# Softmax in a fused image-text block: the row maximum subtracted on VectorE, head by head, in place of one GpSimd operation

## The chip, the cores and the metric

The kernel runs on one core of a Trainium2 chip. The core has five engines that run their own instruction streams and meet only at semaphores: PE (TensorE, matrix products), DVE (VectorE), ACT (ScalarE), POOL (GpSimd) and SP (SyncE, which here only issues transfers). The time is device time in microseconds (us) of one execution; the median of three runs is 970.14 us, the lowest 968.85 and the highest 973.57.

## What is computed

64 samples. Each has 36 image tokens (a patch embedding with shifted copies, then a layer norm) and 77 text tokens, so T = 113 tokens of width 128. One attention layer of 8 heads and one mixture of 16 experts (3 for each token) with a shared expert follow, both with a residual. What matters here is the softmax inside the attention:

```
h = layernorm_patches(x);  h = concat([h, txt], axis=1)            # (64, 113, 128)
q, k, v = projections of layernorm(h), 8 heads of 64
scores = (q * scale) @ k.T        -> bfloat16                       # (64, 8, 113, 113)
probs  = softmax(scores)          -> bfloat16                       # subtract the row maximum, exp, divide
h = h + (probs @ v) @ Wo + bo
h = h + shared_expert(layernorm(h)) + sum over the 3 chosen experts of gate * expert(layernorm(h))
```

## The kernel before, in words

It has three stages. Up to some 120 us the image tokens are made. From some 120 to 620 us a software pipeline runs over the samples, which is the stage of the change. After it, 100 tiles of 256 expert rows are computed and the results are gathered and added.

**The pipeline.** `steps` writes the same step out for each engine: octets of 8 samples, k = 0 to 7 in each, six of the octets in a loop. Sample n = 8 o + k is the one whose softmax stands in the step. In the same step other parts work on other samples: the layer norm of n + 8 (L1137), the projections of n + 4, the scores and v of n + 1, the product of probabilities and v of n - 1 (L715 to L717), the output projection (L687), the residual (L1148) and the second layer norm (L1150, L1161, L498, L500, L1188) of n - 2, the gate of n - 3. Each engine takes its instructions in the order in which they are written, and a wait holds all behind it.

**The softmax of a sample.** ScalarE copies the scores from two PSUM banks into `s16` as bfloat16 (L890, `s_copied`). VectorE takes the maximum of each row and head (L1142, `max_done`). GpSimd subtracts it, all 8 heads in one operation, with the maximum broadcast along a row (L488, `sub_done`). ScalarE takes the exponential into `p16` (L884). TensorE transposes the 8 heads (L650), ScalarE copies them out (L855), and TensorE multiplies by v.

**VectorE's step** in order: xn of n + 8 (L1137); the maximum (L1142); the residual add of n - 2, which waits for TensorE's output projection L687 (L1148); statistics (L1150); a correction of the transposed input (L1155); the statistics' end (L1161); the reciprocal of the softmax sum, which waits for the last product L717 (L1169); the division (L1171); v's remainders (L1177, L1182); the rows to be sent (L1188), which wait for GpSimd's L500. TensorE's L715 waits for L1148, since both use one PSUM bank. Between these stand pieces of the routing: the choice of experts for four samples in the steps with k % 4 == 3 and 0 (L1026 to L1065), their places in the steps with k % 4 == 1 (L1077 to L1088).

**GpSimd's step** in order: the subtraction (L488), a bias add to `h` (L494), the reciprocal root of the second norm (L498, L500, after L1161), and 0, 3, 3, 3, 3, 4, 4, 4 indirect transfers (L533, table `SENDS`), which send the previous octet's rows to their experts. Octet 0 has none of these.

Of the kernel before, what the change touches and what calls it, by code (L numbers as in the profile page):

```python
# [15 lines left out]
BF16 = mybir.dt.bfloat16  # L16
U32 = mybir.dt.uint32
I32 = mybir.dt.int32
ALU = mybir.AluOpType
# [41 lines left out]
def build(nc, x, txt, w_main, w_sx, w_sy, tok_bias, tok_gb, wq, wkv, wo, bo, gate_w, e_bias, w_ffn, out):  # L61
    ctx = ExitStack()
    with ctx:
        def sb(name, shape, dt=FP32):
            return ctx.enter_context(nc.sbuf_tensor(name, shape, dt))
# [76 lines left out]
        v1 = [top_half(vf[i][0:T, :, :]) for i in range(4)]  # L142
        v2 = [top_half(vr[i][0:T, :, :]) for i in range(4)]

        s16 = [sb(f"s16_{i}", [128, H, T], BF16) for i in range(2)]
        p16 = [sb(f"p16_{i}", [128, H, T], BF16) for i in range(2)]
        mx = [sb(f"mx{i}", [128, H], BF16) for i in range(2)]
        pt = [sb(f"pt{i}", [128, H, 128], BF16) for i in range(2)]
        rec = sb("rec", [128, 2, H])

# [90 lines left out]
        def after(eng, name, n, plus=1):  # L241

            if isinstance(n, int) and n + plus <= 0:
                return
            eng.wait_ge(S[name], n + plus)
# [42 lines left out]
        def ok(n, end=B):  # L288

            return not isinstance(n, int) or 0 <= n < end  # L290
# [104 lines left out]
        def _(pool):  # L395
# [84 lines left out]
            def step(o, k):  # L480
                n = o * OCT + k
                if isinstance(o, int) and o == -1 and k in (4, 5):
                    first_rs(NOCT - 2 if k == 4 else NOCT - 1)
                if ok(n):


                    after(pool, "max_done", n)
                    nc.gpsimd.tensor_tensor(s16[k % 2][0:T, :, :], s16[k % 2][0:T, :, :],  # L488
                                            mx[k % 2][0:T, :].unsqueeze(2).to_broadcast([T, H, T]), ALU.subtract).then_inc(S["sub_done"], 1)
                if ok(n + 6):  # L490

                    after(pool, "xn_ready", n + 6)
                    hn = h[0:T, bass.ds(n + 6, 1), :].rearrange("p a d -> p (a d)")
                    nc.gpsimd.tensor_tensor(hn, hn, bo_sb[0:T, :], ALU.add).then_inc(S["hb_done"], 1)  # L494
                if ok(n - 2):

                    after_all(pool, ("ones_set", 5), ("st2_done", n - 2, 1))
                    nc.gpsimd.tensor_scalar(ve2[0:T, k % 2:k % 2 + 1], mv2[0:T, k % 2, 1:2], EPS, None, ALU.add).then_inc(S["ve2_done"], 1)  # L498
                    after(pool, "ve2_done", n - 2)
                    nc.gpsimd.tensor_tensor(rs2[0:T, k % 2:k % 2 + 1], ve2[0:T, k % 2:k % 2 + 1], half[0:T, 0:1], ALU.pow).then_inc(S["rs2_done"], 1)  # L500
                send(o, k, 0)
                send(o, k, 1)

                if ok(n - 7) and k % GRP == GRP - 1:

                    q, half_ring = o * 2 + (k - 7) // GRP, (k - 7) % OCT // GRP
                    at = slice(half_ring * GRP, (half_ring + 1) * GRP)
                    if not isinstance(q, int) or q >= 1:
                        after(pool, "dest_set", 2 * q, 0)
                    for j in range(GRP):  # L510
                        b = half_ring * GRP + j
                        reuse(pool, b, o - 1 if k < 7 else o)
                    nc.gpsimd.tensor_tensor(pay[0:T, at, :, ROW - 1].bitcast(I32), dest_i[0:T, :, :], dzero[0:T, :, :], ALU.add).then_inc(S["dest_set"], 1)
                    after(pool, "dest_set", 2 * q)
                    nc.gpsimd.tensor_tensor(dest_i[0:T, :, :], dest_i[0:T, :, :], dstep[0:T, :, :], ALU.add).then_inc(S["dest_set"], 1)
                send(o, k, 2)
# [44 lines left out]
        def _(pe):  # L561
# [43 lines left out]


            pe.wait_ge(S["z_copied"], NOCT)
            pe.wait_ge(S["pt_zero"], 3)
            pe.wait_ge(S["ones_set"], 5)

            def shared_hidden(g, gate_bank, up_bank):
# [193 lines left out]
        def _(act):  # L805
# [22 lines left out]
                    copies(j * 2 + i, i)  # L828
                    image_rows(act, j * 2 + i - 2, i)

            act.wait_ge(S["pt_zero"], 3)

            def early(g, i):
                if ok(g, NEARLY):
# [4 lines left out]
            def step(o, k):  # L839
# [40 lines left out]
                if ok(n):  # L880

                    after(act, "sub_done", n)
                    after(act, "pt_done", n, -1)
                    nc.scalar.activation(p16[k % 2][0:T, :, :], s16[k % 2][0:T, :, :], ACT.Exp).then_inc(S["exp_done"], 1)  # L884
                if ok(n + 1):

                    after(act, "s_done", n + 1)
                    after(act, "exp_done", n + 1, -1)
                    for i in range(2):
                        m = nc.scalar.activation(s16[(k + 1) % 2][0:T, i:H:2, :], bank[3 + i][0:T, 0:4 * T].rearrange("p (c t) -> p c t", t=T),  # L890
                                                 ACT.Copy)
                    m.then_inc(S["s_copied"], 1)
                if isinstance(o, int) and o == NOCT and k == IDLE:
# [55 lines left out]
        def _(dve):  # L949
# [56 lines left out]
            for i in range(2):  # L1006
                nc.vector.memset(pt[i][:, :, :], 0.0).then_inc(S["pt_zero"], 1)
            nc.vector.memset(bank[5][:, :], 0.0).then_inc(S["pt_zero"], 1)
            dve.wait_ge(S["pt_zero"], 3)
            dve.wait_ge(S["iota_f"], 5)  # L1010

            def per_choice(a):
# [111 lines left out]
            def step(o, k):  # L1124
# [14 lines left out]
                if ok(n):  # L1139

                    after(dve, "s_copied", n)
                    nc.vector.reduce_max(mx[i][0:T, :], s16[i][0:T, :, :], AX.X).then_inc(S["max_done"], 1)  # L1142
                routing(o, k, 0)
                if ok(n - 2):

# [156 lines left out]
```

## Time and profile before

| | |
|---|---|
| median of three runs | 970.14 us |
| the profiled execution | 973.1 us |
| its span | 971.3 us |
| PE busy | 703.8 us (72%) |
| DVE busy | 599.2 us (62%) |
| ACT busy | 440.4 us (45%) |
| POOL busy | 676.2 us (70%) |
| granted TensorE clock, mean | 0.865 |

The profiled execution is one run with the hardware profiler on; its span is the time from its first to its last instruction, and 1.8 us lie around it. Busy is the time in which an engine has at least one instruction in work. The shares are means over stages with different limits, so the stage of the pipeline is read by itself below.

### The profile page before, as it was taken

The numbers are of one execution on the slowest core, as the hardware profiler recorded it, in microseconds if no ns is written. First come the engines' busy times: TensorE is split into PE (matmuls) and PEld (weight loads), VectorE is DVE, ScalarE is ACT, GpSimd is POOL, SyncE is SP. The second block draws the span as 40 slices with busy tenths as digits, with TensorE's granted clock in tenths as the row PEclk, the third lists the DMA queues.
The fourth block names the chain that finished last, engine by engine and source line by source line (L and its number), as shares of the span: only waits on it lengthen the run. The fifth ranks groups of instructions, "written<-read, shape, count | busy, mean of one in ns | idle before, by whom it ended". The sixth has DMA issues, their size and how long they took to land.

```text
span 971.3 us, 21625 instructions
## 1 busy us (share of the span) xinstructions
PE 703.8 (72%) x6192; PEld 578.9 (60%) x6192; DVE 599.2 (62%) x1659; ACT 440.4 (45%) x1027; POOL 676.2 (70%) x782
## 2 busy tenths in 40 slices
PE   3472599987988879888797788589887777877000
PEld 2362377876777768767676677458665655655000
DVE  1197578777887987888778786534333333333095
ACT  2121388666766757666666665214333223332000
POOL 2169354687887887878778777755777777777553
PEclk9686699888998998999899886589999999999555
DMA  7540000000000000000000000157666565663196
GB/s 197 163 136 19 12 1 2 18 26 19 22 27 17 24 27 19 25 19 24 24 19 24 20 24 28 34 169 216 197 185 175 176 184 166 176 182 118 49 349 214
DMA packets 71473, 85.60 MB, mean 88 GB/s; under 512 B 13943, under 2 KB 65152, under 8 KB 71355
## 3 DMA queue, kind: packets, MB, share of 16 engines
q1 hardware_dynamic: 33912, 37.34, 13.5%
q10 hardware_dynamic: 24976, 25.32, 9.4%
q0 software_dynamic: 12544, 22.44, 6.9%
q8 instruction: 19, 0.31, 0.1%
q14 instruction: 22, 0.18, 0.1%
HBM read 55.50 MB, written 31.85 MB: 90 GB/s over the span
## 4 chain that ended last, share of the span: by engine, by line
issue 26%; POOL 24%; PE 18%; DMA 8%; DVE 8%; ACT 1%; POOLq 1%; DVEq 0%; SPq 0%
POOL dispatched L533 8%; POOL expert_rows L546 7%; POOL s L488 6%; DMA expert_rows<-yb,xs_all 5%; PE bank L603 4%; PE bank L687 3%; DMA x2t<-expert_rows 3%; PE bank L735 2%; PE bank L650 2%; PE bank L703 2%; POOL h L494 2%; POOL rs L500 1%; DVE h L1255 1%; PE bank L783 1%; ACT p L884 1%
## 5 line engine op out<-in xcount | busy, mean ns | idle before, releaser
L546 POOL DMA_INDIRECT expert_rows<-yb,xs_all x200 | 194.4, 972 | 73.2 <-issue 51.8
L533 POOL DMA_INDIRECT dispatched<-pay,sloti x192 | 198.3, 1033 | 62.0 <-issue 58.4
L488 POOL TENSOR_TENSOR s<-s,mx 113x904 bf16<-113x904 bf16 x64 | 109.3, 1708 | 45.0 <-DVE mx L1142 44.4
L1243 DVE TENSOR_TENSOR yb<-bank,xs_all 128x256 f32<-128x256 f32 x100 | 42.3, 423 | 142.8 <-DMA expert_rows<-yb,xs_all 140.8
L603 PE MATMUL bank<-xt,wqkv 128*128 128x452 f32 x384 | 114.4, 434 | 1.2 <-DVE xt L1155 0.7
L783 PE MATMUL bank<-xe,kt 128*128 128x256 f32 x400 | 105.3, 386 | 0.1
L921 ACT ACTIVATE xe<-bank 128x256 f32<-128x256 f32 x100 | 38.3, 383 | 140.2 <-PE bank L771 132.9
L792 PE MATMUL bank<-kt,hide 128*128 128x128 f32 x400 | 67.2, 291 | 47.6 <-DVE hide L1233 47.0
L792 PEld LDWEIGHTS bank<-kt,hide 128*128 128x128 f32 x400 | 55.3, 191 | 73.8 <-DVE hide L1233 60.9
L884 ACT ACTIVATE p<-s 113x904 bf16<-113x904 bf16 x64 | 61.3, 957 | 53.8 <-POOL s L488 53.5
L603 PEld LDWEIGHTS bank<-xt,wqkv 128*128 128x128 f32 x384 | 77.5, 220 | 7.3 <-DVE xt L1155 0.9
L650 PE MATMUL bank<-ident,p 113*113 113x113 bf16 x512 | 42.8, 232 | 46.7 <-ACT p L884 46.6
L687 PEld LDWEIGHTS bank<-wo_r,ot 128*113 128x113 f32 x512 | 72.8, 211 | 5.7 <-ACT ot L850 2.0
L783 PEld LDWEIGHTS bank<-xe,kt 128*128 128x128 f32 x400 | 68.8, 192 | 7.1 <-issue 0.7
L687 PE MATMUL bank<-wo_r,ot 128*113 128x128 f32 x512 | 70.4, 288 | 1.5 <-ACT ot L850 1.5
L1142 DVE TENSOR_REDUCE mx<-s 113x8 bf16<-113x904 bf16 x64 | 69.5, 1087 | 2.2 <-ACT s L890 1.9
L735 PE MATMUL bank<-kt,qt 64*113 64x113 f32 x1024 | 70.5, 279 | 0.0
L703 PE MATMUL bank<-wqkv,xt 128*113 128x512 f32 x192 | 66.1, 456 | 0.1
L650 PEld LDWEIGHTS bank<-ident,p 113*113 113x113 bf16 x512 | 35.1, 143 | 51.6 <-ACT p L884 51.2
L715 PEld LDWEIGHTS bank<-vf,pt 113*128 113x128 bf16 x512 | 49.1, 101 | 26.5 <-issue 26.5
L735 PEld LDWEIGHTS bank<-kt,qt 64*113 64x113 f32 x1024 | 58.8, 183 | 8.0 <-issue 2.1
L890 ACT ACTIVATE s<-bank 113x452 bf16<-113x452 f32 x128 | 62.4, 543 | 2.6 <-PE bank L735 2.4
(161 smaller groups left out, 1799.4 us busy)
## 6 DMA issues: line engine op xcount, KB each, us to landing
kt<-in_w_ffn ACTq DMA_DIRECT2D x100, 192.0 KB
xs_all<-dispatched SPq DMA_DIRECT2D x100, 130.0 KB, 2.5
x2t<-expert_rows SPq DMA_DIRECT2D x16, 672.0 KB
x2t<-in_x SPq DMA_DIRECT2D x8, 864.0 KB, 5.6
out_h<-h ACTq DMA_DIRECT2D x16, 224.0 KB
expert_rows<-yb,xs_all POOLq DMA_INDIRECT x200, 2.3
dispatched<-pay,sloti POOLq DMA_INDIRECT x192, 2.3
h<-in_txt SPq DMA_DIRECT2D x1, 2464.0 KB
```

The costliest lines, as they stand in the source:

```text
L488: nc.gpsimd.tensor_tensor(s16[k % 2][0:T, :, :], s16[k % 2][0:T, :, :], mx[k % 2][0:T, :].unsqueeze(2).to_broadcast([T, H, T]), ALU.subtra ...
L533: pool.indirect_dma_start(out=xs_dram[:, :], out_offset=bass.IndirectOffsetOnAxis(ap=sloti[:, b // GRP, b % GRP, c:c + 1], axis=0), in_=pa ...
L546: pool.indirect_dma_start(out=y_dram[:, :], out_offset=bass.IndirectOffsetOnAxis(ap=xs[slot][:, j, ROW - 1:ROW].bitcast(I32), axis=0), in_ ...
L603: m = nc.tensor.matmul(dst, wqkv[:, a, at:at + 128], xg[:, b, :], start=(j == 0), stop=(j == 2))
L650: m = nc.tensor.transpose(ptp[0:T, hh * 128:hh * 128 + T], p16[(k - 1) % 2][0:T, hh, :], ident16[0:T, 0:T])
L687: m = nc.tensor.matmul(bank[7][0:T, 0:D], ot[k % 2][:, c, :], wo_r[:, a, c * D:(c + 1) * D], start=(c == a == 0), stop=(c == NC - 1 and a ...
L703: m = nc.tensor.matmul(bank[1][0:T, :], xt[gv][:, b, kv * T:(kv + 1) * T], wqkv[:, a, 2 * H * DH:], start=(j == 0), stop=(j == 2))
L735: m = nc.tensor.matmul(bank[3 + e][0:T, c * T:(c + 1) * T], qt[gs][half_p, c, ks * T:(ks + 1) * T], kt[gs][half_p, c, ks * T:(ks + 1) * T] ...
L783: m = nc.tensor.matmul(bank[3 - i][:, j * TR:(j + 1) * TR], w_ex[slot][:, j * F:(j + 1) * F], xe[1 - i][:, :], start=True, stop=True)
L792: m = nc.tensor.matmul(bank[4 + i][:, j * D:(j + 1) * D], hide[i][:, j * 128:(j + 1) * 128], w_ex[(k - 2) % RW][:, 2 * F:], start=True, st ...
L884: nc.scalar.activation(p16[k % 2][0:T, :, :], s16[k % 2][0:T, :, :], ACT.Exp).then_inc(S["exp_done"], 1)
L1142: nc.vector.reduce_max(mx[i][0:T, :], s16[i][0:T, :, :], AX.X).then_inc(S["max_done"], 1)
```

## The change

The scores' tile gets 114 columns for each head instead of 113, and column 113 is set to zero once ahead of the pipeline. The row maximum is kept as 32-bit numbers. GpSimd's subtraction goes. In its place VectorE, after the maximum and a wait for it, issues eight operations, one for each head, on 113 partitions and 114 bfloat16 elements, with the head's maximum as a scalar of each partition. The last of them signals `sub_done`. ScalarE's copies and exponential leave the added column out.

```
-        s16 = [sb(f"s16_{i}", [128, H, T], BF16) for i in range(2)]
+        s16 = [sb(f"s16_{i}", [128, H, TP], BF16) for i in range(2)]
-        mx = [sb(f"mx{i}", [128, H], BF16) for i in range(2)]
+        mx = [sb(f"mx{i}", [128, H]) for i in range(2)]
...
-                if ok(n):
-                    after(pool, "max_done", n)
-                    nc.gpsimd.tensor_tensor(s16[k % 2][0:T, :, :], s16[k % 2][0:T, :, :],
-                                            mx[k % 2][0:T, :].unsqueeze(2).to_broadcast([T, H, T]), ALU.subtract).then_inc(S["sub_done"], 1)
...
-                    nc.scalar.activation(p16[k % 2][0:T, :, :], s16[k % 2][0:T, :, :], ACT.Exp).then_inc(S["exp_done"], 1)
+                    nc.scalar.activation(p16[k % 2][0:T, :, :], s16[k % 2][0:T, :, 0:T], ACT.Exp).then_inc(S["exp_done"], 1)
...
+            for i in range(2):
+                nc.vector.memset(s16[i][:, :, T:TP], 0.0).then_inc(S["pt_zero"], 1)
...
-                    nc.vector.reduce_max(mx[i][0:T, :], s16[i][0:T, :, :], AX.X).then_inc(S["max_done"], 1)
+                    nc.vector.reduce_max(mx[i][0:T, :], s16[i][0:T, :, 0:T], AX.X).then_inc(S["max_done"], 1)
+                    after_all(dve, ("txt_in", 16), ("max_done", n, 1))
+                    for hh in range(H):
+                        m = nc.vector.tensor_scalar(s16[i][0:T, hh, :], s16[i][0:T, hh, :], mx[i][0:T, hh:hh + 1], None, ALU.subtract)
+                    m.then_inc(S["sub_done"], 1)
```

VectorE, the step k = 2 in the loop over octets, before (xn, mx and h are the tiles of the text above, bank is PSUM, s_0 is a scores' tile):

```order
L1137 TENSOR_SCALAR xn<-h,mean,rs 113x128
L1142 TENSOR_REDUCE mx<-s_0 113x8 [waits s_copied]
L1148 ISA [waits hb_done,y_done]
L1148 TENSOR_TENSOR h<-bank,h 113x128
L1150 BN_STATS st<-h 113x6 [waits h_done,txt_in]
```

and the same place now, where the maximum is line 1138 and xn line 1133, and L1148 has kept its number:

```order
L1133 TENSOR_SCALAR xn<-h,mean,rs 113x128
L1138 TENSOR_REDUCE mx<-s_0 113x8 [waits s_copied]
L1141 TENSOR_SCALAR s_0<-s_0,mx 113x114 [waits max_done,txt_in]
L1141 TENSOR_SCALAR s_0<-s_0,mx 113x114 x7
L1148 ISA [waits hb_done,y_done]
L1148 TENSOR_TENSOR h<-bank,h 113x128
L1150 BN_STATS st<-h 113x6 [waits h_done,txt_in]
```

The eight new operations stand between the maximum and the residual add L1148, for which TensorE's L715 waits; nothing else on the engine has moved.

GpSimd, the step k = 2 in the same loop, before (ve and rs are the second norm's root, dispatched is the experts' input in memory):

```order
L488 TENSOR_TENSOR s_0<-s_0,mx 113x904 [waits max_done]
L245 REGISTER_ALU
L494 ISA [waits xn_ready]
L494 TENSOR_TENSOR h<-h,bo_sb 113x128
L498 TENSOR_SCALAR ve<-mv 113x1 [waits st2_done,ones_set]
L500 TENSOR_TENSOR rs<-ve,half 113x1 [waits ve2_done]
L533 DMA dispatched<-pay,sloti 120064x130 x3
```

and now:

```order
L488 ISA [waits xn_ready]
L488 TENSOR_TENSOR h<-h,bo_sb 113x128
L249 REGISTER_ALU
L492 TENSOR_SCALAR ve<-mv 113x1 [waits st2_done,ones_set]
L494 TENSOR_TENSOR rs<-ve,half 113x1 [waits ve2_done]
L527 DMA dispatched<-pay,sloti 120064x130 x3
```

The subtraction with its wait for the maximum is gone, and what followed it follows the transfers of the step before directly.

## Rows read from the trace of the kernel before

**Rows 1.** Timeline of GpSimd, one step: start us, us, engine, operation.

```profile
413.84 1.71 POOL L488 TENSOR_TENSOR s<-s,mx 113x904 bf16<-113x904 bf16 x1
415.49 0.47 POOL L494 TENSOR_TENSOR h<-h,bo_sb 113x128 f32 x1
...
417.41 1.21 POOL L533 DMA_INDIRECT dispatched<-pay,sloti  x1 [0.20 <-issue]
...
423.23 1.71 POOL L488 TENSOR_TENSOR s<-s,mx 113x904 bf16<-113x904 bf16 x1
```

**Rows 2.** Timeline of GpSimd, the subtractions with k = 0, octets 2 and 7.

```profile
234.94 1.72 POOL L488 TENSOR_TENSOR s<-s,mx 113x904 bf16<-113x904 bf16 x1
...
550.57 1.72 POOL L488 TENSOR_TENSOR s<-s,mx 113x904 bf16<-113x904 bf16 x1
```

**Rows 3.** Waits of ScalarE, 290 to 560 us: total us, times, longest.

```profile
ACT p L884 <- POOL s L488: 41.0, 23, 3.5
```

**Rows 4.** Windows: each engine's busy us, (x instructions), granted clock, DMA share, GB/s.

```profile
154.90:160.73 5.83, 5.83 (x76) 5.09 (x74) 4.74 (x12) 5.11 (x14) 2.86 (x4) 1.00 0.01 3
250.00:550.00 300.00, 251.75 (x2876) 215.50 (x2874) 249.36 (x697) 203.19 (x458) 243.50 (x289) 0.93 0.07 23
```

**Rows 5.** Timeline of VectorE, a step of octet 0, without transfers.

```profile
155.14 0.29 DVE L1148 TENSOR_TENSOR h<-bank,h 113x128 f32<-113x128 f32 x1 [0.32 <-PE bank L687]
...
156.81 0.21 DVE L1169 RECIPROCAL rec<-bank 113x8 f32<-113x8 f32 x1 [0.71 <-PE bank L717]
...
159.31 0.33 DVE L1137 TENSOR_SCALAR xn<-h,mean,rs 113x128 f32<-113x128 f32 x1
159.56 1.09 DVE L1142 TENSOR_REDUCE mx<-s 113x8 bf16<-113x904 bf16 x1
160.56 0.19 DVE L1026 TENSOR_SCALAR wz<-tbias 113x64 f32<-113x64 f32 x1
160.97 0.29 DVE L1148 TENSOR_TENSOR h<-bank,h 113x128 f32<-113x128 f32 x1 [0.22 <-PE bank L687]
```

**Rows 6.** Timeline of VectorE, a step of octet 4.

```profile
403.20 0.29 DVE L1148 TENSOR_TENSOR h<-bank,h 113x128 f32 x1 [0.17 <-PE bank L687]
...
404.64 0.21 DVE L1169 RECIPROCAL rec<-bank 113x8 f32<-113x8 f32 x1 [0.48 <-PE bank L717]
```

**Rows 7.** Groups of VectorE, 250 to 550 us: x count, busy us, mean ns, idle before.

```profile
L1182 DVE TENSOR_TENSOR v<-vr 113x512 bf16<-113x512 f32 x39 | 38.2, 978 | 0.0
...
L1177 DVE TENSOR_TENSOR vr<-bank,vf 113x512 f32<-113x512 f32 x39 | 26.3, 675 | 0.0
...
L1082 DVE TENSOR_TENSOR wz<-wz 113x192 f32<-113x192 f32 x9 | 9.2, 1022 | 0.0
L1040 DVE CAST topf<-topi 113x12 f32<-113x12 uint32 x10 | 8.2, 823 | 0.0
...
L1029 DVE TENSOR_TENSOR wz<-wz,eb_sb 113x64 f32<-113x64 f32 x10 | 6.9, 693 | 0.0
...
L1050 DVE TENSOR_TENSOR wz<-wz 113x192 f32<-113x192 f32 x10 | 3.5, 348 | 0.0
...
L1059 DVE TENSOR_SCALAR gsum<-gsum 113x4 f32<-113x4 f32 x10 | 3.3, 333 | 0.3
...
L1062 DVE RECIPROCAL gsum<-gsum 113x4 f32<-113x4 f32 x10 | 1.7, 166 | 0.0
```

**Rows 8.** Groups of VectorE, whole span, short operations with one source.

```profile
L995 DVE CAST wo_r<-qt 128x512 fp32r<-128x512 f32 x1 | 0.4, 416 | 0.0
L1214 DVE TENSOR_SCALAR tgb<-iota_t,last 16x100 f32<-16x100 f32 x1 | 0.3, 260 | 0.0
...
L1221 DVE TENSOR_SCALAR xs_all<-wz 1x100 int32<-1x100 f32 x1 | 0.2, 200 | 0.0
```

**Rows 9.** Timeline of VectorE, eight short operations in a row.

```profile
65.58 0.64 DVE L963 BATCH_NORM_AGGREGATE mv<-st 113x2 f32<-113x6 f32 x8
```

**Rows 10.** Timeline of VectorE, L1137 beside the transfer of rows 1.

```profile
418.14 0.51 DVE L1137 TENSOR_SCALAR xn<-h,mean,rs 113x128 f32 x1 [0.34 <-issue]
```

More of the change, by code:

```diff
@@ L607, in _ @@
             pe.wait_ge(S["z_copied"], NOCT)
-            pe.wait_ge(S["pt_zero"], 3)
+            pe.wait_ge(S["pt_zero"], 5)
             pe.wait_ge(S["ones_set"], 5)
@@ L829, in _ @@
                     image_rows(act, j * 2 + i - 2, i)
-            act.wait_ge(S["pt_zero"], 3)
+            act.wait_ge(S["pt_zero"], 5)
             def early(g, i):
@@ L889, in step @@
                     for i in range(2):
-                        m = nc.scalar.activation(s16[(k + 1) % 2][0:T, i:H:2, :], bank[3 + i][0:T, 0:4 * T].rearrange("p (c t) -> p c t", t=T),
+                        m = nc.scalar.activation(s16[(k + 1) % 2][0:T, i:H:2, 0:T], bank[3 + i][0:T, 0:4 * T].rearrange("p (c t) -> p c t", t=T),
                                                  ACT.Copy)
@@ L1008, in _ @@
             nc.vector.memset(bank[5][:, :], 0.0).then_inc(S["pt_zero"], 1)
-            dve.wait_ge(S["pt_zero"], 3)
+            for i in range(2):
+                nc.vector.memset(s16[i][:, :, T:TP], 0.0).then_inc(S["pt_zero"], 1)
+            dve.wait_ge(S["pt_zero"], 5)
             dve.wait_ge(S["iota_f"], 5)
```

## The prediction

> **What bounds the kernel now.** I read the timeline of GpSimd in the pipeline first. In a step with four transfers GpSimd runs without a pause: the subtraction of sample n, 1.71 us, starts at 413.84, the bias add, the root and four transfers of about a microsecond each follow, and the next subtraction starts at 423.23, the moment the last transfer is out [rows 1]. The maximum that it needs lies ready long before. So the subtraction is late because GpSimd is full. The list of waits says who pays: ScalarE's exponential waited 41.0 us for L488 between 290 and 560 us, 23 times, up to 3.5 us at once [rows 3]. From the subtraction of k = 0 in octet 2 to that in octet 7 there are 315.63 us [rows 2], 63.1 us for an octet and 7.9 us for a step.
>
> The second view is that of windows. In octet 0, where nothing is sent, a step takes 5.83 us with TensorE busy all of it at full clock, and VectorE is busy 4.74 us; between 250 and 550 us VectorE is busy 249.36 us of 300 and GpSimd 243.50 [rows 4]. So three engines stand close together: TensorE needs 5.83 us a step, GpSimd 7.9, and VectorE, which is to take the work, is at 6.6. The question is what VectorE's own round costs once the work is on it.
>
> The third view is VectorE's timeline, for that round. L1148 frees the bank in which TensorE then multiplies by v, and L1169 waits for this product: 1.44 us from L1148 to L1169 where TensorE is not itself late [rows 6]. From L1169 to the end of the maximum VectorE has no gap, 156.81 to 160.65, 3.84 us [rows 5]. Then L1148 of the next step follows; in octet 0 it waits for TensorE's L687, 0.22 to 0.32 us [rows 5]. Without routing the round is 1.44 + 3.84 = 5.28 us, and the new operations are put into it, between the maximum and L1148.
>
> **What is removed.** 64 subtractions of 1.71 us on GpSimd. Per octet that is 13.7 us, which leaves GpSimd at most 63.1 - 13.7 = 49.4 us an octet. The exponential's wait goes too: its input is ready when L1148 starts, ahead of the product with v, and ScalarE reaches the exponential after it. What is late next is VectorE.
>
> **What is added.** A wait for the maximum and eight operations, in every step. The wait costs the overlap of two instructions and the signal: L1142 starts at 159.56 and takes 1.09, the next starts at 160.56, 0.09 before its end; behind a signal an instruction starts some 0.1 us after the end instead. That is 0.19 us.
>
> No row shows a subtraction of a scalar from bfloat16 data. I build one. L995 takes 416 ns for 512 elements and L1221 200 ns for 100 [rows 8]: 0.52 ns an element, and 148 ns fixed. L1214, as long as L1221 but with its scalar read for each partition, takes 260 [rows 8]: 60 ns for the scalar. If 16-bit elements go at twice the rate, 114 of them take 30 ns: 0.24 us each. L1137 takes 0.33 and its successor starts 0.25 after it [rows 5], so the pitch is the duration less 0.08 to 0.09: 0.155 us. Eight make 1.24 us, with the wait 1.43 us a step.
>
> The bounds: eight short operations of six elements take 0.64 us [rows 9], a pitch of 0.066, and with 30 ns for the elements and nothing for the scalar 0.095. Above, L1137 itself, 128 elements with two scalars, has a pitch of 0.25 [rows 5]; the same comes out if the elements go at the rate of the maximum, 904 in 1.09 us less the fixed part, 1.04 ns each. A new operation can't cost less than nothing on VectorE, and the eight lie in the round, so the ends are 0.76 and 2.0 us for the eight. I take 1.24, since L1214 is the nearest in form: one source, one scalar of each partition.
>
> **What VectorE gets back.** Its operations with two inputs are held while GpSimd's operations run: L1182 takes 978 ns in the mean, its twin L1177, which reads PSUM, 675; L1082 takes 1022 where L1050 of the same size takes 348; L1040 takes 823 where a short one like L1062 takes 166; L1029 takes 693 where 64 elements take 190 [rows 5, 7]. That is 39 x 0.303 + 9 x 0.674 + 10 x 0.657 + 10 x 0.503 = 29.5 us; L1059 and two groups like it, 28 instructions with some 0.167 each, add 4.7 [rows 7]. Together 34.2 us in 300, or 4.75 octets: 7.2 us an octet. I give all of it to the subtraction, and count what stays under contention.
>
> The page SBUF — State Buffer of the Trainium skill, section Who interferes with whom, says that VectorE and GpSimd share one pair of ports as a lock, that whoever starts first keeps it for its whole instruction, and that scalar operations on 16- and 32-bit data in SBUF ask for it. For GpSimd's tensor operations the trace agrees (978 against 675 ns). For its transfers it does not: L1137 beside a 1.21 us transfer took 0.51 instead of 0.33.
>
> **Contention that is new.** The eight operations now stand where GpSimd is sending. Beside a transfer L1137 lost 0.51 - 0.33 = 0.18 us [rows 5, 10]; once in each of the seven steps that send, 1.3 us. GpSimd's bias add takes 0.47 us [rows 1] and now comes straight behind the last transfer, about 5.8 us after L1148, on the new operations; I count it in three steps of eight, 1.4 us. Together 2.7 us an octet.
>
> **The sum for an octet with transfers.** VectorE busy 249.36 / 4.75 = 52.5; less 7.2, 45.3. The wait for the product stays only in the two steps without routing, 2 x 0.48 [rows 6] = 1.0; small gaps behind signals, 0.15 a step, 1.2. That is 47.5. The new work is 8 x 1.43 = 11.4, contention 2.7: 61.6 us against 63.1, 1.5 less. GpSimd's 49.4 and TensorE's 8 x 5.83 = 46.6 with the routing's few products are below it, so VectorE is the bound. Octets 1 to 6: 9.0 us gained. In octet 7 part of the work is missing on all engines, and I count it even.
>
> **Octet 0 loses.** There TensorE is the bound at 5.83 us. VectorE's round becomes 5.28 + 1.43 = 6.71: 0.88 more in five steps, and 0.5 in the step with routing, 4.9 us. The two memsets ahead of the pipeline, the stage of the experts and the gathering cost or gain nothing: what ends the pipeline there is the last octet's 24 transfers, which stay.
>
> 9.0 - 4.9 = 4.1 us gained. On the profiled execution (span 971.3, 973.1 in all) that is 969.0. This execution lies 3 us above the median of the runs, so against the median 970.14 it is **966 us**.
>
> The sum is a small difference of large terms. One tenth of a microsecond in the pitch is 0.8 us a step and, over the 54 steps of octets 0 to 6 in which VectorE is the bound, 43 us. The kernel is as fast as before at a pitch of 0.165 us, and slower by 0.5% from 0.176. I take 0.5% (4.9 us) as what a measurement of this kernel can tell from no change.
>
> **The rivals.**
>
> First, short operations: reading the scalar hides behind the operation in front, and the pitch is 0.095. For it speaks the row of eight at 0.066, against it L1137's 0.25 for 128 elements, which has no other reason to be that long. 0.48 us less a step, 54 steps: 26 us, 940 us. VectorE stays the bound at 57.8 us an octet.
>
> The page Vector Engine (DVE) Microarchitecture Reference of the Trainium skill, section 5.2, gives about 75 ns for an instruction in a row beside its elements. By it the eight would cost 8 x (0.075 + 0.030) = 0.84 us, and the kernel would take some 944 us, an estimate from that page. The trace agrees for the operations without a scalar of each partition (0.066 for six elements), and no row shows eight with one.
>
> Second, the slower side, long operations: the elements go one at a time, or the scalar costs more than L1214 shows, and the pitch is 0.25 as with L1137. The place is the block between the maximum and L1148, its price 0.7 us a step, and it decides from 0.165. For it speaks L1137, an operation of the same kind and length; against it its second scalar and its 32-bit data. 39 us more: 1005 us. Half way, at 0.2, it is 985.
>
> Third, the lock: where the block meets a transfer, one of the eight waits for nearly the whole of it. Each of seven steps loses 0.8 us more than I count, 5.6 us an octet, 34 us: 1000 us. Against it stands L1137's loss of 0.18.
>
> Fourth, that the change does not free the exponential: VectorE's new operations would have to end after ScalarE reaches it. They end ahead of L1148, some 1.5 us before the product with v is done. I give it nearly nothing.
>
> **How the numbers follow.** The forecast (pitch 0.13 to 0.18) 0.47, short operations 0.21, long operations 0.20, the lock 0.10, the rest 0.02. The forecast's own range is 950 to 985. The whole range takes in most of both sides: 942 to 1003. Faster by over 0.5%: 0.4 of the forecast's 0.47 (0.19), nearly all of the first rival (0.20), 0.01 of the rest, 0.40. Within 0.5%: 0.17 of the forecast and 0.04 of the others, 0.21. Slower: 0.11 of the forecast, 0.19 and 0.09 of the second and third rival, 0.39.
>
> **What would show it.** The new operations' mean and the distance of their starts, 0.24 and 0.155; L1182 near 0.68 and L1082 near 0.35; no wait of the exponential for the subtraction; TensorE's L715 waiting for L1148 in nearly every step; steps in octet 0 of 6.7 instead of 5.83 us; GpSimd waiting for L1161 in most steps; an octet of 61.6 us. I am wrong if the pitch is outside 0.13 to 0.18, if L1182 stays near 0.98 (then the transfers or the bias add held it, and up to 7 us an octet come back), or if the octets are set by TensorE at half clock.

## The result, and the profile after

The changed kernel takes 967.33 us (median of 13 runs, 963.76 to 971.81), the kernel before beside it 972.06 us (13 runs, 968.85 to 973.59): a ratio of 0.9954, with a 95% interval of 0.9935 to 0.9972, 4.5 us less by the ratio. The sign does not hold everywhere: on a third chip, where the kernel before takes 1051.92 us, the changed one takes 1.020 of it (below); on a second chip the changed kernel was not run as it stands. What follows explains the gain on the first chip and then what eats it.

The profiled run of the changed kernel, 971.81 us, is the slowest of its thirteen. Its span, 970.0, is only 1.3 us shorter than before's; from the first maximum of the pipeline to the last it takes 474.9 us against 481.5. The other 5.3 us lie outside the pipeline, 1.5 ahead of the first maximum (122.1 against 120.6) and 3.9 behind the last (373.1 against 369.2 to the end), and both stretches vary as much among the other kernels on this chip, whose work there is the same (120.7 to 122.1, 369.5 to 373.6). Timelines are therefore compared step by step. First, the page's chain of the work that ended last:

```profile
DVE 36%; issue 19%; PE 11%; DMA 9%; POOL 9%; DVEq 1%; ACT 1%; POOLq 1%; SPq 0%; ACTq 0%
```

VectorE carries the chain now. GpSimd's share fell from 24% to 9%.

Windows: a stretch of octet 0 as long as a step was before, and 250 to 550 us, with columns as in [rows 4].

```profile
149.06:154.90 5.84, 5.23 (x61) 4.47 (x60) 5.60 (x19) 5.04 (x12) 0.85 (x2) 1.00 0.01 3
250.00:550.00 300.00, 244.95 (x2869) 209.67 (x2868) 279.52 (x1009) 201.94 (x463) 175.64 (x257) 0.96 0.07 24
```

In octet 0 TensorE was busy all of its 5.83 us before; now it pauses. In the long window VectorE goes from 249.36 to 279.52 of 300 us, GpSimd from 243.50 to 175.64.

VectorE's timeline, one step of octet 0 (before: [rows 5]):

```profile
151.61 1.09 DVE L1138 TENSOR_REDUCE mx<-s 113x8 f32<-113x904 bf16 x1
152.81 1.37 DVE L1141 TENSOR_SCALAR s<-s,mx 113x114 bf16<-113x114 bf16 x8
154.09 0.28 DVE L1148 TENSOR_TENSOR h<-bank,h 113x128 f32<-113x128 f32 x1
...
155.46 0.21 DVE L1169 RECIPROCAL rec<-bank 113x8 f32<-113x8 f32 x1 [0.42 <-PE bank L711]
...
158.21 1.09 DVE L1138 TENSOR_REDUCE mx<-s 113x8 f32<-113x904 bf16 x1
```

The block is one row, x8. From its start to the next instruction's start there are 1.28 us, 0.160 for each operation, and the step is 158.21 - 151.61 = 6.60 us. The only wait for another engine left in the round is that for the product with v.

The groups of VectorE between 250 and 550 us (before: [rows 7]) and the waits between 290 and 560 us (before: [rows 3]):

```profile
L1141 DVE TENSOR_SCALAR s<-s,mx 113x114 bf16<-113x114 bf16 x312 | 63.8, 300 | 4.2
...
L1182 DVE TENSOR_TENSOR v<-vr 113x512 bf16<-113x512 f32 x39 | 27.0, 692 | 0.0
...
L1036 DVE CAST topf<-topi 113x12 f32<-113x12 uint32 x10 | 3.3, 326 | 0.0
...
L1078 DVE TENSOR_TENSOR wz<-wz 113x192 f32<-113x192 f32 x9 | 3.1, 349 | 0.0
...
L1025 DVE TENSOR_TENSOR wz<-wz,eb_sb 113x64 f32<-113x64 f32 x10 | 2.2, 215 | 0.0
```

```profile
POOL ve L492 <- DVE mv L1161: 80.1, 30, 7.5
...
PE bank L709 <- DVE h L1148: 34.9, 25, 2.2
...
DVE h L1148 <- PE bank L681: 2.8, 3, 1.2
```

L1182 came down from 978 to 692 ns, the groups of 1022, 823 and 693 to 349, 326 and 215. GpSimd, TensorE and ScalarE now wait for VectorE or for what hangs on it; the exponential's 41.0 us for the subtraction are gone. VectorE waits for TensorE's L681 three times only.

From the maximum of one octet's first step to that of the next octet, octets 0 to 7 (seven steps in the last), from the timelines, in us:

```
before 46.2 63.3 62.5 63.5 62.2 64.7 62.0 57.1
after  50.7 61.7 62.5 63.4 61.8 62.0 60.7 52.1
```

### The profile page after: what moved, and what is told of

It is laid out like the page before. It is cut to its first block, busy times and chain, and to the rows that moved or that the text cites. A ratio compares the mean times of both kernels' runs of the same rounds, so it can differ in the third digit from the quotient of the medians.

```text
span 970.0 us, 22139 instructions
## 1 busy us (share of the span) xinstructions
PE 688.6 (71%) x6192; PEld 564.5 (58%) x6192; DVE 648.3 (67%) x2173; ACT 435.7 (45%) x1027; POOL 558.3 (58%) x718
## 4 chain that ended last, share of the span: by engine, by line
DVE 36%; issue 19%; PE 11%; DMA 9%; POOL 9%; DVEq 1%; ACT 1%; POOLq 1%; SPq 0%; ACTq 0%
DVE s L1141 9%; POOL expert_rows L540 6%; DVE mx L1138 6%; DMA expert_rows<-yb,xs_all 6%; DVE v L1182 3%; DMA x2t<-expert_rows 3%; DVE pay L1188 3%; DVE vr L1177 2%; POOL dispatched L527 2%; PE bank L729 2%; DVE xn L1133 1%; PE bank L777 1%; PE bank L709 1%; PE bank L597 1%; DVE h L1148 1%
## 5 line engine op out<-in xcount | busy, mean ns | idle before, releaser
L527 POOL DMA_INDIRECT dispatched<-pay,sloti x192 | 195.9, 1020 | 62.2 <-issue 56.9
L492 POOL TENSOR_SCALAR ve<-mv 113x1 f32<-113x1 f32 x64 | 14.7, 230 | 171.2 <-DVE mv L1161 171.2
L597 PE MATMUL bank<-xt,wqkv 128*128 128x452 f32 x384 | 104.1, 403 | 1.2 <-DVE xt L1155 0.7
L1141 DVE TENSOR_SCALAR s<-s,mx 113x114 bf16<-113x114 bf16 x512 | 100.1, 288 | 6.9
L709 PE MATMUL bank<-vf,pt 113*128 113x65 bf16 x512 | 57.8, 200 | 60.2 <-DVE h L1148 60.2
L786 PEld LDWEIGHTS bank<-kt,hide 128*128 128x128 f32 x400 | 55.3, 191 | 75.8 <-DVE hide L1233 60.4
L597 PEld LDWEIGHTS bank<-xt,wqkv 128*128 128x128 f32 x384 | 70.9, 201 | 6.8 <-DVE xt L1155 0.9
L729 PE MATMUL bank<-kt,qt 64*113 64x113 f32 x1024 | 73.9, 288 | 0.0
L1138 DVE TENSOR_REDUCE mx<-s 113x8 f32<-113x904 bf16 x64 | 69.4, 1085 | 2.3 <-ACT s L884 1.9
L681 PEld LDWEIGHTS bank<-wo_r,ot 128*113 128x113 f32 x512 | 62.6, 185 | 5.8 <-ACT ot L844 3.1
L681 PE MATMUL bank<-wo_r,ot 128*113 128x128 f32 x512 | 61.7, 265 | 2.5 <-ACT ot L844 2.5
L849 ACT ACTIVATE pt<-bank 113x912 bf16<-113x912 bf16 x64 | 61.6, 962 | 1.3 <-PE bank L644 0.4
```

The source lines that it names most:

```text
L527: pool.indirect_dma_start(out=xs_dram[:, :], out_offset=bass.IndirectOffsetOnAxis(ap=sloti[:, b // GRP, b % GRP, c:c + 1], axis=0), in_=pa ...
L597: m = nc.tensor.matmul(dst, wqkv[:, a, at:at + 128], xg[:, b, :], start=(j == 0), stop=(j == 2))
L681: m = nc.tensor.matmul(bank[7][0:T, 0:D], ot[k % 2][:, c, :], wo_r[:, a, c * D:(c + 1) * D], start=(c == a == 0), stop=(c == NC - 1 and a ...
L709: nc.tensor.matmul(dst[:, at:at + DH + 1], probs, v1[(k - 1) % 4][:, hh, :], start=True, stop=False)
L729: m = nc.tensor.matmul(bank[3 + e][0:T, c * T:(c + 1) * T], qt[gs][half_p, c, ks * T:(ks + 1) * T], kt[gs][half_p, c, ks * T:(ks + 1) * T] ...
L786: m = nc.tensor.matmul(bank[4 + i][:, j * D:(j + 1) * D], hide[i][:, j * 128:(j + 1) * 128], w_ex[(k - 2) % RW][:, 2 * F:], start=True, st ...
```

## Experiments

The kernels of the first group ran on the first chip, beside the kernel before at 971.47 us. The second group ran on a second chip (before 1055.66 us), the third on a third (before 1051.92 us). These two chips take about 455 us from the last maximum to the end, where the first takes about 370, so there only ratios and the pipeline's steps are compared.

**First chip: what the tile's padding costs.** `e1`: GpSimd's operation put back, the 114 columns and the 32-bit maximum kept.

```
+    nc.gpsimd.tensor_tensor(s16[..][0:T, :, 0:T], .., mx.. to_broadcast, ALU.subtract)
-    for hh in range(H): nc.vector.tensor_scalar(..)
```

> The subtraction is back on GpSimd as one operation; the tile of 114 columns and the 32-bit maximum stay. Theory (what moved the time is who subtracts): as the kernel before, ratio to it 1.000 within 0.3%, octets of 63.1 us, octet 0 with steps of 5.83 us. Rival (the wider tile or the 32-bit maximum costs something by itself on ScalarE or VectorE): more than 0.5% away from the kernel before, with ScalarE's copy into s or its exponential longer than 543 and 957 ns.

971.41 us, ratio 0.9995 (0.9977 to 1.0014), octets as before except octet 1 (60.6 instead of 63.3). The padding and the 32-bit maximum move the time by no more than 0.23%, half of the gain; the gain belongs to the move.

**What the scalar of each partition costs.** `e4`: the constant in place of `mx[i][0:T, hh:hh + 1]`.

> The eight operations subtract the constant 4.0 in place of the row maximum, so the subtraction of the maximum is left out; all waits stay. Theory (VectorE's round is the bound, and the scalar of each partition costs 60 ns an operation): the pitch falls from 0.161 to 0.10 us, 0.49 us a step less, over some 55 steps 27 us: 940 us, ratio to the kernel before 0.967. Rival 1 (the scalar is free and the pitch is made of something else): pitch 0.16, 967 us. Rival 2 (VectorE's round is not what sets the steps): the pitch falls and the time stays at 967 us.

934.0 us, ratio 0.9617 (0.9601 to 0.9633). Its timeline of VectorE in octet 0:

```profile
150.88 0.89 DVE L1141 TENSOR_SCALAR s<-s 113x114 bf16<-113x114 bf16 x8
151.69 0.28 DVE L1148 TENSOR_TENSOR h<-bank,h 113x128 f32<-113x128 f32 x1
```

0.81 us for eight, 0.101 each. Reading a scalar for each partition costs 0.059 us an operation, 0.47 a step, 64 steps 30 us, and the kernel is 33 us below the changed one. The prediction counted 43 us for 0.1 us in the pitch, which is 25 for 0.059; with every step following VectorE it is 30, and 3 more come with it. So the pitch moves the time, by a third more than was counted.

**What an operation costs beside its elements.** `e5`: each of the eight cut into 56 and 58 columns.

```
+    for c in (slice(0, 56), slice(56, TP)):
+        m = nc.vector.tensor_scalar(s16[i][0:T, hh, c], .., mx[i][0:T, hh:hh + 1], ..)
```

> Each of the eight operations is cut in two, 56 and 58 columns: the same elements, sixteen operations. Theory (VectorE's round is the bound and nearly all of an operation is fixed): pitch 0.145 us, the block 2.3 instead of 1.3 us, 1.0 us more in some 55 to 60 steps: 1022 to 1028 us, ratio to the kernel before 1.055. Rival (elements make the price): pitch 0.08, under 975 us. Rival 2 (there is slack in VectorE's round): the block grows to 2.3 us and the time by less than 30 us.

1061.28 us, ratio 1.092 (1.0897 to 1.0944): more than expected.

```profile
150.73 2.41 DVE L1142 TENSOR_SCALAR s<-s,mx 113x56 bf16<-113x56 bf16 x16
153.04 0.29 DVE L1149 TENSOR_TENSOR h<-bank,h 113x128 f32<-113x128 f32 x1
```

2.31 us for sixteen, 0.144 each. With 0.160 for 114 elements and 0.144 for 57 that makes some 0.28 ns an element and 0.128 us for the rest. The block grew by 1.03 us, 66 us in 64 steps; 28 of the 94 us are more than that. The window of 170 to 550 us has TensorE's granted clock at 0.82:

```profile
170.00:550.00 380.00, 301.75 (x3076) 259.34 (x3074) 341.62 (x1392) 220.45 (x493) 175.35 (x259) 0.82 0.06 19
```

It is 0.95 in the changed kernel. I take the rest for steps of TensorE at the lower level; no run holds the clock fixed, so this is argued and not shown.

**Who holds the block.** On the changed kernel's timeline, GpSimd beside VectorE:

```profile
311.66 0.99 POOL L527 DMA_INDIRECT dispatched<-pay,sloti  x1 [0.30 <-issue]
...
312.96 0.97 POOL L527 DMA_INDIRECT dispatched<-pay,sloti  x1 [0.30 <-issue]
...
313.31 1.82 DVE L1141 TENSOR_SCALAR s<-s,mx 113x114 bf16<-113x114 bf16 x8
...
313.95 0.49 POOL L488 TENSOR_TENSOR h<-h,bo_sb 113x128 f32 x1
```

Of 18 blocks between 289 and 424 us, the five that meet only transfers or nothing take 1.37 us, as in octet 0; the thirteen that meet the bias add take 1.57 to 1.84. A window that holds only the first operation of the block above shows that the delay begins ahead of the add:

```profile
313.31 0.65 DVE L1141 TENSOR_SCALAR s<-s,mx 113x114 bf16<-113x114 bf16 x1
```

It takes 0.65 us instead of 0.25 and ends as the transfer ends and the add starts; the rest is lost beside the add. Why the tail of a transfer counts when an add follows it, and not otherwise, is not shown. `e7` issues the bias add behind the root, ahead of the transfers:

```
     nc.gpsimd.tensor_tensor(rs2.., ve2.., half.., ALU.pow)
+    if ok(n + 6): .. nc.gpsimd.tensor_tensor(hn, hn, bo_sb[0:T, :], ALU.add)
     send(o, k, 0)
```

> GpSimd's bias add (0.47 us) is moved from the start of its step to behind the root (ve, rs) and ahead of the transfers, so that it falls on VectorE's reads of PSUM and not on the eight subtractions. Theory (the eight are held by this bias add, 1.82 instead of 1.37 us in most steps, and not by the transfers): the block is 1.37 us everywhere, an octet 2.6 us shorter, 18 us in all: 949 us, ratio to the kernel before 0.977. Rival 1 (the transfers hold them): the block stays at 1.6 to 1.8 us in most steps, 967 us. Rival 2 (the add holds another operation of VectorE instead): the block is 1.37 us, and the division, v's remainder or the rows to be sent grow by the same 0.45 us, 967 us.

960.63 us, ratio 0.9904 (0.9881 to 0.9928).

```profile
307.10 0.45 POOL L494 TENSOR_TENSOR h<-h,bo_sb 113x128 f32 x1
...
310.45 1.38 DVE L1141 TENSOR_SCALAR s<-s,mx 113x114 bf16<-113x114 bf16 x8
...
310.48 0.98 POOL L527 DMA_INDIRECT dispatched<-pay,sloti  x1 [0.30 <-issue]
```

The block is 1.37 to 1.42 in all steps but one (1.50), with transfers beside it. The add, behind a transfer, was the holder. But the 18 us were too much from the start: in the changed kernel the blocks of octets 1 to 6 are 1.7 to 2.6 us an octet longer than eight of 1.37, those of octet 7 0.5, together 12.6 us. Of these 5 reach the end by the ratios and 7 by the medians. The second rival falls: the division, v's remainder and the rows to be sent take 692, 681 and 541 ns, against 691, 692 and 547 in the changed kernel. What grew is VectorE's wait for TensorE's L681, from 2.1 to 6.7 us between 250 and 550 us. The profiled execution, 955.88 us, is the fastest of its four; its octets 1 to 6 take 60.5, 60.9, 61.8, 60.9, 59.0 and 58.6 us, and in the longer ones stand steps with TensorE's granted clock between 0.75 and 0.83: k = 1 takes 8.9 us at 0.81 and 7.6 at full clock, k = 5 takes 9.1 at 0.79 and 7.6 at full clock. A part of VectorE's saving is spent there.

**Second chip: half the heads left with GpSimd.** `e2`: `for hh in range(4)` on VectorE, heads 4 to 7 in one operation on GpSimd.

> Heads 0 to 3 are subtracted by VectorE (four operations), heads 4 to 7 by GpSimd (one operation), both behind the maximum; the exponential waits for both. Theory (GpSimd's tensor operations and VectorE's scalar operations exclude each other, and GpSimd reaches its half late because it is sending): the four take 0.7 us alone but GpSimd's 0.87 us is added where they meet or falls on v's remainder, and the exponential waits again: 960 to 985 us, ratio to the kernel before 0.99 to 1.01. Rival (the engines work side by side and only VectorE's count of operations matters): 0.64 us a step less than with eight, 35 us: 932 us, ratio 0.96.

1108.61 us, ratio 1.0475 (1.0396 to 1.0553), worse than either theory. Two groups between 250 and 550 us:

```profile
L1146 DVE TENSOR_SCALAR s<-s,mx 113x114 bf16<-113x114 bf16 x132 | 55.4, 493 | 3.5
```

```profile
L486 POOL TENSOR_TENSOR s<-s,mx 113x452 bf16<-113x452 bf16 x33 | 31.7, 960 | 20.4 <-DVE mx L1143 19.6 <-issue 0.5
```

VectorE's four take 493 ns in the mean instead of 248: 4 x 0.245 = 1.0 us, the whole of GpSimd's 0.96. Both start at the same signal, and VectorE waits out GpSimd: the block is 1.70 us in octet 0, and 0.73 in the steps in which GpSimd comes to its half later. Nothing is shared by splitting: a step of octet 0 takes 6.91 us, 0.32 more than with eight on VectorE. Octets 1 to 5 are 71.3 to 71.9 us; a part of that is the stall of this chip in the step k = 6, of which more below.

**One operation instead of eight.** `e3`:

```
+    nc.vector.tensor_tensor(s16[i][0:T, :, 0:T], s16[i][0:T, :, 0:T],
+                            mx[i][0:T, :].unsqueeze(2).to_broadcast([T, H, T]), ALU.subtract)
```

> VectorE subtracts all eight heads in one operation with two inputs, 904 elements, the maximum broadcast along a row, at the place of the eight. Theory (VectorE's round is the bound, the price of the eight is their fixed part): it takes as long as the maximum over the same 904 elements, 1.09 us, 0.29 us less a step than the eight: 16 us, 951 us, ratio to the kernel before 0.979. Rival 1 (16-bit elements go two at a time): 0.6 us, 926 us. Rival 2 (an operation with two inputs is held longer by GpSimd's bias add and gives the gain back): 967 us.

1055.5 us, ratio to before 0.9995 (0.9953 to 1.0037), not the 0.979 of the theory. Steps of octet 0 are 6.32 us, 0.27 below the changed kernel's 6.59, near the 0.29 of the theory. How much of the miss is the second rival and how much is the chip can only be told on a chip that runs the changed kernel too (`e12`).

```profile
303.06 1.10 DVE L1140 TENSOR_TENSOR s<-s,mx 113x904 bf16<-113x904 bf16 x1
...
310.43 1.42 DVE L1140 TENSOR_TENSOR s<-s,mx 113x904 bf16<-113x904 bf16 x1
...
311.06 1.09 POOL L488 TENSOR_TENSOR h<-h,bo_sb 113x128 f32 x1
```

Where the bias add meets it, it takes 1.42, and the add 1.09 instead of 0.49: here both are held.

**The block moved** behind the changed kernel's L1161, where VectorE waited for the product with v (there the block itself has the line L1161). `e6`:

> The wait and the eight operations stand behind L1161 (the end of the statistics) instead of ahead of the residual add L1148, in the stretch in which VectorE waits for the product with v. Theory (GpSimd's ve and rs, 0.22 and 0.57 us, come at that moment and hold the eight; TensorE no longer waits for L1148 but the exponential comes late): the block takes 1.9 to 2.2 us, 967 to 990 us, ratio to the kernel before 0.995 to 1.02. Rival (what costs time is only that the eight stand in front of L1148): the wait of 0.41 us for the product is filled in two steps of eight and in octet 0, the block stays at 1.4 us: 957 us, ratio 0.985.

1056.71 us, ratio 1.0033 (0.9989 to 1.0077). That is in the theory's range, but not for its reason. Octet 0 is 6.3 us a step; the block takes 1.34 us in most steps, and 1.63 or 1.64 in five of octet 0, in which its last operation meets the bias add. GpSimd's root, 0.57 us on one column, holds none of the 241 operations that it meets alone:

```profile
L1161 DVE TENSOR_SCALAR s<-s,mx 113x114 bf16<-113x114 bf16 x304 | 52.9, 252 | 0.0
```

```profile
PE bank L636 <- DVE o L1172: 32.1, 38, 1.8
...
DVE h L1144 <- PE bank L681: 18.9, 19, 1.6
```

The waits are those between 250 and 550 us. TensorE waits for L1172, late behind the block, and VectorE for TensorE's L681, for which it waits 2.1 us in this window in the changed kernel. That these waits form a ring which takes back what was spared is my reading; the stall of this chip is in this run too, and no run of the changed kernel on this chip separates the two.

**113 columns** instead of 114, `e8`:

> The eight operations work on 113 of the 114 columns (the tile keeps 114). Theory (an operation is nearly all fixed part, and the odd count does not change how the elements are read): 1.37 us a block, 967 us, ratio to the changed kernel 1.000. Rival (the even count is what lets four elements go in a clock; with 113 they go one or two at a time, 0.03 or 0.09 us more an operation): a block of 1.6 or 2.1 us, 980 or 1006 us.

1071.76 us, ratio 1.014 (1.008 to 1.0201). Steps of octet 0 6.58 us, the operation's mean 302 ns against 300: the odd width costs nothing. That leaves its octets of 64 to 65 us unexplained, and asks for the changed kernel on such a chip.

**Third chip: two by two.** The changed kernel again (`e10`), both edits (`e9`), the early bias add (`e11`), the single operation (`e12`).

> The changed kernel once more, so that the three kernels that follow can be set against it on one chip. Expected 0.995 of the kernel before, with steps of 6.59 us in octet 0 and octets of 61 to 63 us. If the changed kernel itself shows long k = 6 and k = 7 steps (8.3 and 9.2 us, as the 113-column kernel did) wherever the chip grants TensorE half its clock there, those steps belong to TensorE's clock and not to the width of the tile.

1069.47 us, ratio 1.0197 (1.0169 to 1.0225). The 0.995 expected fails. That the long steps belong to the chip and not to the width holds; that they belong to TensorE's clock does not: k = 6 takes 8.2 us in octets 2 and 4 with the clock at 1.00.

> Both edits together: one tensor_tensor over 904 columns (1.10 us where nothing holds it) in place of the eight (1.37 and 1.82), and GpSimd's bias add issued ahead of its transfers. My theory, that VectorE's round is the bound and GpSimd's tensor op is what stretches it: 0.29 us less in every step and some 2.6 us less in every octet, 64 x 0.29 + 7 x 1.5 = 18.6 + 10.5 = 29 us below the changed kernel if every step follows VectorE, some 940 us on a chip where the kernel before takes 971 (0.968 of it). Rival, TensorE's clock: what VectorE is spared is spent where TensorE runs at half clock, so that the second edit gives little on top of the first; then no more than 12 us below the changed kernel, 0.983 to 0.99 of the kernel before.

1039.94 us, ratio 0.9889 (0.9837 to 0.9941): 29.5 us below the changed kernel, where the first theory said 29. The best of all: it beats both kernels there, though 0.968 of before does not come, because the changed kernel starts from 1.020. That 29.5 meets 29 is in part luck: octets 2 to 6 of the profiled runs are 28.1 us shorter than the changed kernel's, where the theory gives 5 x 3.8 = 19, and 12.5 of the 28.1 are in the steps k = 6 and 7, in which the stall below stands. Octet 1 is 1.4 us longer.

> The early bias add with the eight operations, on the same chip as the changed kernel. Earlier it stood at 0.990 of the kernel before. Expected 0.990 again, and against the changed kernel of this chip 0.993 to 0.997; octets of 59 to 61 us.

1067.91 us, ratio 1.017 (1.0132 to 1.0208): 1.6 us below the changed kernel, no more. What `e7` won on the first chip is not won here; the clock is 0.89 between 170 and 550 us, against 0.93.

> The single tensor_tensor with the bias add where it was, on the same chip as the changed kernel. Octet 0 at 6.31 us per step. If the saving of 0.29 us per step reached the end, 18 us under the changed kernel, 0.977 of the kernel before; if TensorE's clock or GpSimd's hold takes it, within 6 us of the changed kernel, 0.990 to 1.0.

1053.75 us, ratio 1.002 (0.9982 to 1.0058): 15.7 us below the changed kernel, near the 18 of the first theory. The level against before was missed for the same reason. The bias add's place is worth 1.6 us with the eight operations and 13.8 with the one.

Windows of 250 to 550 us, first of `e10`, then of `e9`:

```profile
250.00:550.00 300.00, 246.36 (x2762) 207.96 (x2762) 269.22 (x957) 197.51 (x446) 166.96 (x242) 0.93 0.07 22
```

```profile
250.00:550.00 300.00, 253.42 (x3017) 213.91 (x3015) 270.20 (x762) 210.37 (x482) 183.01 (x263) 0.99 0.08 24
```

In `e9` TensorE is at 0.99, and octets 2 to 6 take 58.8 to 60.4 us.

**What makes the changed kernel slower on the third chip.** From the first maximum to the last it takes 489.0 us there and 474.9 on the first chip. The octets 1 to 6 are 64.0 to 65.9 us, and octet 0 (6.59 us a step) and the steps k = 0 to 5 are like those of the first chip (k = 1 to 5: 7.6 or 8.1, 7.0, 8.4, 7.7, 8.0 on both). The step k = 6 takes 8.2 to 9.1 us instead of 6.58, and k = 7 8.8 to 9.5 instead of 8.28; over octets 2 to 6 these two steps are 13.5 us longer together, and the other six 1.2. The step k = 6 of octet 2 in `e10`, all engines:

```profile
285.94 0.48 POOL L488 TENSOR_TENSOR h<-h,bo_sb 113x128 f32 x1
286.85 0.27 ACT L863 ACTIVATE xt<-bank 128x113 fp32r<-128x113 f32 x1 [1.73 <-remote]
286.93 0.29 DVE L1148 TENSOR_TENSOR h<-bank,h 113x128 f32 x1 [1.53 <-remote]
...
287.34 0.10 PEld L709 LDWEIGHTS bank<-vf,pt 113*128 113x128 bf16 x1 [2.38 <-issue]
287.37 0.19 PE L709 MATMUL bank<-vf,pt 113*128 113x65 bf16 x1 [1.96 <-DVE h L1148]
```

ScalarE and VectorE wait for two different results of TensorE (L691, L681). By the records these were done at 284.3, and the waits end together at 286.9; "remote" says that the profile has no releaser. On the first chip ScalarE does not wait there, and VectorE once, with a releaser. Between 280 and 290 us only GpSimd's DMA queue has packets, so no load of code shows. Such waits go with the chip and not with an edit. Between the first and the last maximum, the six traces of the first chip have none without a releaser; each of the eight of the other two chips has 15 to 36, up to 2.6 us long, in most octets in the step k = 6. In octets 2 to 6 of `e9` only ScalarE has one there (1.2 us, L867), VectorE none, and the step takes 7.2 or 7.3 us. What the stall is stays open. So does whether the kernel before has it: its trace was not taken on these chips. If its way from the last maximum to the end were the 455 us of the others, its pipeline would take some 475 us there, no more than on the first chip, as if it had no stall; that is an estimate.

## Why the prediction was right, and where only its sum was

**The block.** Foreseen 0.155 us a pitch and 1.43 us a step. Measured 0.160; from the maximum's start to L1148's there are 2.48 us, 1.48 more than the 1.00 from the maximum to its successor before [rows 5]. Its parts came out one by one: eight without a scalar 0.101, less 114 x 0.28 ns = 0.032, leaves 0.069, near the 0.066 of [rows 9]; the scalar adds 0.059, where L1214 less L1221 said 0.060 [rows 8]; an element costs some 0.28 ns where 0.26 was taken. The mean of a free operation is 248 ns, 240 foreseen. The first rival left the scalar out, the second took L1137, which has two. (The second rival's price was added up too low: a pitch of 0.25 is 0.76 us a step more, 41 us in 54 steps, not 0.7 and 39.)

The Trainium skill, Vector Engine (DVE) Microarchitecture Reference, section 5.2, gives about 75 ns an instruction in a row, which made 0.105 us an estimate for each. With a constant the trace agrees, 0.101; with a scalar of each partition it does not, 0.160.

**Octet 0.** Foreseen 6.71 us a step and 4.9 us lost; measured 6.59 and 4.5.

**What VectorE gets back.** Foreseen 7.2 us an octet. L1182 at 692 ns, L1078 at 349, L1036 at 326 and L1025 at 215 give 39 x 0.286 + 9 x 0.673 + 10 x 0.497 + 10 x 0.478 = 27.0 us in 4.8 octets against the 29.5 counted of the same four groups. L1036 kept 0.16 of its delay. The three small groups give 4.6 (L1055, L1061 and L1084 at 170, 174 and 173 ns). That makes 6.5 us an octet. By VectorE's busy time without the block, (279.52 - 63.8) / 4.84 = 44.6 us an octet against the 45.3 foreseen, it is 7.9. The window holds no whole number of octets, so 7.2 stands within what it can tell.

**Contention.** Foreseen 2.7 us an octet, measured 2.0 in the mean (1.7 to 2.6), and half of the 2.7 had a wrong reason. I gave 1.3 to the transfers and 1.4 to the bias add in three steps of eight. The transfers cost the block nothing (1.37 us with and without them); the bias add meets it in four to seven steps of eight, five in the mean, for 0.2 to 0.47 us. L1137's 0.51 us beside a transfer [rows 10] I misread as a loss. The row behind it in the trace of before is

```profile
418.40 1.09 DVE L1142 TENSOR_REDUCE mx<-s 113x8 bf16<-113x904 bf16 x1
```

The next instruction starts 0.26 us after L1137, against 0.25 without a transfer [rows 5]. And of the 41 times that L1137 stands beside a transfer in that trace, it takes 0.33 us in 34. The third rival, the lock against transfers, falls with this reading.

The Trainium skill, SBUF — State Buffer, Who interferes with whom, has a lock that the first holder keeps for its whole instruction. For GpSimd's operations on whole tiles the runs agree nearly (0.45 us for an add of 0.49; 1.0 us for one of 0.96). Its indirect transfers and its one-column root do not hold the block.

**The octets.** Foreseen 61.6 against 63.1, 9.0 us in six; measured 62.0 against 63.0, 6.2 us. The pitch adds 0.3 us to the octet (64 x 0.005), contention takes 0.7 less than foreseen, and one term was at nothing: steps in which TensorE is below its full clock. Eight steps of octets 1 to 6 with a granted clock of 0.70 to 0.89 are 5.7 us longer than steps of the same k at full clock, such as the one of 8.53 us at 0.79 in octet 3 against 8.04: some 1.0 us an octet, an estimate. Together that makes 62.2. Octet 6, all at full clock, takes 60.7 us.

**Octet 7.** Counted even, it gave 5.0 us. Its last three steps took 24.8 us before with TensorE's granted clock at 0.50, 0.50 and 0.60, and 22.2 after at 0.79, 0.58 and 1.00; the other 2.5 us are in its first four, at GpSimd's pace before. `e1` has before's pattern.

So +4.5 - 6.2 - 5.0 = -6.7 us on the pipeline stand for the foreseen +4.9 - 9.0 = -4.1, and -4.5 (2.7 to 6.3) for the whole kernel by the ratio. The mechanism and the size of the block were right. That the sum came within 1 us of this is in part luck: the octets gave 2.8 us less than foreseen and octet 7, counted even, 5.0 more, and not all that the profiled pipeline gained stands in the medians.

**What the prediction had no term for** is the chip. "The octets are set by TensorE at half clock" was named as what would make it wrong, and on the first chip it is a small part. On the third chip the changed kernel is 2% above before, with a stall in its pipeline that was in none of the rivals; whether the kernel before has this stall there is not shown.

## What to carry to other kernels

Price a new VectorE operation in parts, each from a row: the fixed pitch, the elements, the scalar of each partition; with eight in a block the scalar alone was worth some 30 us here, and one operation over all columns was the cheaper form (1.10 us against 1.37). Look what stands beside the block on GpSimd: a whole-tile operation of 0.49 us cost VectorE nearly all of its length, an indirect transfer nothing. Moving the former ahead of the latter freed the block, but only 5 to 7 us of 12.6 reached the end on the first chip and 1.6 us on the third, and on the first VectorE then waited for TensorE. A gain of half a per cent is worth a run on a second chip before it is believed, and the kernel before belongs into that run's profile too.

## What the runs showed of the hardware that was not expected

- A scalar read for each partition adds 0.059 us to each VectorE operation on 114 bfloat16 columns (pitch 0.160 against 0.101), and an odd column count of 113 nothing (302 against 300 ns).
- GpSimd's indirect transfers leave a block of such operations alone (1.37 us beside two of them), and so does its root on one column (none of 241 operations held, `e6`). Its bias add on 113x128 does not (1.82).
- TensorE's granted clock does not simply follow VectorE's load. Between 250 and 550 us it is 0.82 with sixteen operations, 0.96 and 0.93 in the changed kernel on the first and third chip, and 0.99 with both edits; but with the early bias add alone, which spares VectorE too, it falls to 0.94 and 0.88.
- The two other chips need 1.08 to 1.09 of the first one's time for the kernel before, and the same edit changes its sign between two of them: 0.9954 on the first, 1.0197 on the third. Waits whose releaser the profile does not show stand in the pipeline of all eight traces of the two slower chips and of none of the six of the first.
